# Attention without V: normalised probabilities on the input's rows, and one folded matrix per head

## The chip, the cores and the metric

One core of a Trainium2 chip runs the whole program. The metric is the device time of one execution in microseconds; smaller is better. Three runs of the kernel before took 1573.14 to 1573.82 us, 1573.54 in the median.

## The reference

The program is two layers on 8 sequences (batches) of 512 tokens of 128 features, in float32. Layer 0 is a Mamba block times the SiLU of a mixture of 24 experts. Layer 1, which the change touches, is causal attention times the SiLU of a mixture of 128 experts. Cut to the attention, per batch:

```python
xn = x / max(|x|, 1e-12) * sqrt(128) * gamma          # rows of 512 tokens
q, k, v = split(xn @ w_qkv.T)                         # 8 heads of 128
sim = (q * 128**-0.5) @ k.T                           # causal mask above the diagonal
attn = softmax(sim, axis=-1)
out = concat_heads(attn @ v) @ w_out.T                # 128 features again
```

As everything is linear in v, a head's share of `out` is attn @ xn @ (Wv.T Wo.T): the product of the two weight matrices can be made once per head.

## The kernel before

Layer 1 has two stages. `attention_input_stage` normalises the rows of x, scales them (`xa`, in a ring of four batches), transposes them (`xaT`, where gamma is multiplied in) and folds the weights on TensorE: M holds per head Wq.T Wk scaled by 128**-0.5, N holds per head Wv.T Wo.T. Both are 128 x 1024.

`attention_stage` then runs 64 heads (n = 8 b + h), in a loop on each engine that is written out by hand. An engine works strictly in the order of its own program; semaphores join the engines. For head n:

- TensorE `query(n)` makes M_h.T xaT in the bank `p_q` (two heads ahead); ScalarE `copy_query` takes it to `qT`.
- TensorE `score(n)` makes four tiles of rows against 128, 256, 384 or 512 keys, with the mask added by a bfloat16 product, in the order of `BANKS`: tile 3, then tiles 2 and 0, then tile 1.
- VectorE `maxima(n)` takes each tile's negated maximum; ScalarE `exps(n)` writes `pr` and the row sums (`sums`).
- TensorE `turn(n)` transposes the ten 128x128 blocks in three parts into two banks `p_t` (with `query(n + 2)` between the second and the third, which reuses the first part's bank); VectorE copies the parts to `pT`.
- TensorE `weigh(n)` makes the head's output in `p_o`: ten products of 128 columns, with blocks of pT as weights and V as the moving side. V is made by `value(k)` eight heads ahead, one 128x512 product per head through `p_q` (and `p_s` for the first eight, ahead of the first query), and copied by ScalarE (`copy_value`).
- VectorE `add_head(n)`, one head later, multiplies `p_o` by the reciprocal of the sums and adds it to `s_rows`. It counts `out_used`, for which the next `weigh` waits.

In float32 one product is two matmul instructions in the trace; a transpose is one.

Beside each loop runs the work of `Moe1` (`side_by_side`): at each `yield` of the main loop the engine takes one step of it. There are two yields per head. TensorE has them after `turn(n)` and after `score(n + 1)`, ScalarE after `exps(n)` with the copy behind it and after `copy_query(n + 2)`, and VectorE ahead of the copies to pT and ahead of `maxima(n + 1)`. So VectorE's order for head n is: maxima(n), side step, copies(n), add_head(n - 1), side step, maxima(n + 1). By step number the side work is: steps 0 to 15 `leaders` (the two best experts), 15 to 30 counting, 32 to 39 the one-hot tables, 40 the gates, 44 to 75 the expert products (TensorE, ScalarE), 84 to 107 `combine` on VectorE in two of three steps, 110 the SiLU of 4096 rows on ScalarE, and from 114 on, in every second step, one batch of the output: two 128x512 products on VectorE (`s_rows_added` is `out_used`), and its store. GpSimd makes masks and running counts beside steps 0 to 18 and issues the gathers later.

Of the kernel before, what the change touches and what calls it, by code (L numbers as in the profile page):

```python
# [24 lines left out]
P = 128  # L25
# [1652 lines left out]
NH = 8  # L1678
# [7 lines left out]

def attention_input_stage(nc, w, xn_dram, x_rows, xn_rows, xaT, M, N, loads):


    with ExitStack() as ctx:  # L1690
# [6 lines left out]
        xnT = s.sb("xnT", [P, 2, L])  # L1697
        xa = s.sb("xa", [P, 4, TB, D])
        qkv = s.sb("qkv", [P, 3 * NH, D])
# [47 lines left out]
        def _(dve):  # L1747
            link = Chain(dve, chain)
            v = nc.vector
            for g in range(B + 4):  # L1750
# [16 lines left out]
                if 2 <= g <= B + 1:  # L1767
                    b = g - 2
                    t = tiles(b)
                    dve.wait_ge(norm_ready, b + 1)  # L1770
                    link(v.tensor_scalar(l2[:, t], l2[:, t], 1e-12, float(D) ** -0.5, ALU.max, ALU.mult))
                    link(v.reciprocal(l2[:, t], l2[:, t]))
                    dve.wait_ge(normed, b + 1)
                    if b >= 4:
                        dve.wait_ge(a_turned, b - 3)
                    v.tensor_tensor(xa[:, b % 4, :, :], xn_rows[:, tiles(b), :], bcast(l2[:, tiles(b)], D),
                                    ALU.mult).then_inc(xa_ready, 1)
# [9 lines left out]
        def _(pe):  # L1787
# [8 lines left out]
            def turn_scaled(b):  # L1796
                pe.wait_ge(xa_ready, b + 1)
                if b >= 2:
                    pe.wait_ge(xaT_ready, b - 1)
                for j in range(TB):  # L1800
                    ins = nc.tensor.transpose(p_a[:, b % 2, j * P:(j + 1) * P], xa[:, b % 4, j, :], w["ident"])
                ins.then_inc(a_turned, 1)
# [34 lines left out]
        def _(act):  # L1837
            for g in range(B + 3):
# [33 lines left out]
def attention_stage(nc, w, xaT, M, N, s_rows, beside):  # L1872

# [4 lines left out]
    with ExitStack() as ctx:  # L1878
        s = Scope(nc, ctx, "at")
        qT = s.sb("qT", [P, 3, L])  # L1880
        V = s.sb("V", [P, 2, TB, NH * D])
        pr = s.sb("pr", [P, 2, 3, 512])
# [9 lines left out]
        q_copied = s.sem("q_copied")  # L1892
        v_product = s.sem("v_product")
        v_copied = s.sem("v_copied")
        scores = s.sem("scores")
        maxed = s.sem("maxed")
        exped = s.sem("exped")
        turned = s.sem("turned")
        pT_ready = s.sem("pT_ready")
# [8 lines left out]

        def value_bank(k):

            return p_s[:, k % 4, :] if k < NH and k % 4 < 3 else p_q[:, :]

        def tensor_steps(pe):
            def query(n):
                b, h = divmod(n, NH)
                pe.wait_ge(v_copied, min(NH * B, NH + max(n - 2, 0)))
                if n:
                    pe.wait_ge(q_copied, n)
                nc.tensor.matmul(p_q[:, :], M[:, h * D:(h + 1) * D], xaT[:, b, :], start=True,  # L1919
                                 stop=True).then_inc(q_product, 1)  # L1920

            def value(k):
                b, i = divmod(k, NH)
                t, half = divmod(i, 2)
                if k >= NH:
                    pe.wait_ge(v_copied, k)
                    pe.wait_ge(q_copied, min(NI, k - NH + 3))
                elif k >= 4:
                    pe.wait_ge(v_copied, k - 3)
                nc.tensor.matmul(value_bank(k), xaT[:, b, t * P:(t + 1) * P], N[:, half * 512:(half + 1) * 512],  # L1930
                                 start=True, stop=True).then_inc(v_product, 1)

# [33 lines left out]

            def weigh(n):
                b, h = divmod(n, NH)
                pe.wait_ge(v_copied, NH * (b + 1))
                if n:  # L1970
                    pe.wait_ge(out_used, n)
                pe.wait_ge(pT_ready, 3 * (n + 1))
                for i in range(TB):
                    for j in range(i + 1):
                        bank, c = PT_AT[j]
                        ins = nc.tensor.matmul(p_o[:, i, :], pT[:, n % 2, bank, c + (i - j) * P:c + (i - j + 1) * P],  # L1976
                                               V[:, b % 2, j, h * D:(h + 1) * D], start=(j == 0), stop=(j == i))
                ins.then_inc(out_ready, 1)

            for k in range(NH):  # L1980
                value(k)
            query(0)
            query(1)
            score(0)
            for n in range(NI):
                turn(n)
                yield
                if n + 1 < NI:
                    score(n + 1)
                yield  # L1990
                if n + NH < NI:
                    value(n + NH)
                weigh(n)

        def scalar_steps(act):
# [5 lines left out]

            def copy_value(k):
                b, i = divmod(k, NH)
                t, half = divmod(i, 2)
                act.wait_ge(v_product, k + 1)
                if b >= 2:
                    act.wait_ge(out_ready, NH * (b - 1))
                nc.scalar.activation(V[:, b % 2, t, half * 512:(half + 1) * 512], value_bank(k),
                                     ACT.Copy).then_inc(v_copied, 1)

            def exps(n):
                if n >= 2:
                    act.wait_ge(turned, 3 * (n - 1))
                if n >= 3:
                    act.wait_ge(out_used, n - 2)
                for k, tiles in enumerate(BANKS):
# [7 lines left out]

            for k in range(NH):
                copy_value(k)
            copy_query(0)
            copy_query(1)
            for n in range(NI):
                exps(n)  # L2030
                if n and n - 1 + NH < NI:
                    copy_value(n - 1 + NH)
                yield
                if n + 2 < NI:
                    copy_query(n + 2)
                yield

        def vector_steps(dve):
# [11 lines left out]

            def add_head(n):
                b, h = divmod(n, NH)
                link(v.reciprocal(sums[:, n % 3, :], sums[:, n % 3, :]))  # L2053
                dve.wait_ge(out_ready, n + 1)
                for i in range(TB):
                    o = s_rows[:, b * TB + i, :]
                    if h == 0:
                        ins = v.tensor_scalar(o, p_o[:, i, :], sums[:, n % 3, i:i + 1], None, ALU.mult)
                    else:
                        ins = v.scalar_tensor_tensor(out=o, in0=p_o[:, i, :], scalar=sums[:, n % 3, i:i + 1], in1=o,  # L2060
                                                     op0=ALU.mult, op1=ALU.add)
                ins.then_inc(out_used, 1)
# [39 lines left out]
class Moe1:  # L2102
# [262 lines left out]
    def vector(self, dve):  # L2365
# [111 lines left out]
        for b in range(B):  # L2477
            t = slice(b * TB, (b + 1) * TB)
            dve.wait_ge(self.g_ready, b // 2 + 1)
            dve.wait_ge(self.s_rows_added, NH * (b + 1))  # L2480
            link(v.tensor_tensor(self.o[:, t, :], self.o[:, t, :], self.s_rows[:, t, :], ALU.mult))
# [19 lines left out]
def program(nc, a, out):  # L2501

    with ExitStack() as top:
# [70 lines left out]
        with ExitStack() as l1:  # L2574
# [7 lines left out]
            w["qkv_dram"], w["wo_dram"] = a["qkv"], a["wo"]  # L2582
            A_ = Scope(nc, l1, "att")
            xaT = A_.sb("xaT", [P, B, L])
            M = A_.sb("M", [P, NH * D])
            N = A_.sb("N", [P, NH * D])
            attention_input_stage(nc, w, xn1_dram, rows, xn_rows, xaT, M, N, l1w)
            with ExitStack() as att:
                moe = Moe1(nc, att, w, r, xn_rows, xn1_dram, a["we"], y3_dram, s_rows, rows, out, outputs_stored)
                attention_stage(nc, w, xaT, M, N, s_rows, moe)  # L2590

# [75 lines left out]
```

## Time and profile before

| | us |
|---|---|
| median of three runs | 1573.54 |
| span of the profiled execution | 1568.1 |
| TensorE matmuls busy | 1331.6 (85%) |
| VectorE busy | 1253.2 (80%) |
| ScalarE busy | 848.2 (54%) |
| GpSimd busy | 650.5 (41%) |
| first instruction of the attention stage | 1027.07 |
| the 64 heads, from first transposes to the end | 1042.2 to 1568.1 |

The profiled execution gives no time of its own beside its span. In the attention stage TensorE is busy 522 of 541 us, at a granted clock of 0.99 to 1.00. A share that high over a stage says little about one head; the order of time within single heads says which engine the next one waits for.

### The profile page before, as it was taken

What the parts mean: (1) busy time and instruction counts of PE and PEld (TensorE: products, weight loads), DVE (VectorE), ACT (ScalarE), POOL (GpSimd) and SP (SyncE); (2) the same over time, 40 slices, a digit from 0 to 9 for tenths busy, and PEclk for the clock granted to TensorE, in tenths of its full rate; (3) what the DMA queues carried; (4) which work ended last, traced back from release to release, by engine and by line L of the source; (5) the groups of instructions that cost most, each with busy time, mean ns of one, the idle gap of its engine ahead of it and who ended that gap; (6) DMA issues with size and microseconds to landing.
All of it is one profiled execution on the core that took longest, in us unless ns stands there. A gap on an engine that the chain in (4) does not pass through costs nothing. (4 is left out here: it accounts for less than half of the span.)

```text
span 1568.1 us, 21870 instructions
## 1 busy us (share of the span) xinstructions
PE 1331.6 (85%) x7560; PEld 909.2 (58%) x7560; DVE 1253.2 (80%) x2263; ACT 848.2 (54%) x2090; POOL 650.5 (41%) x600
## 2 busy tenths in 40 slices
PE   7968788878987757899895696489999999999998
PEld 5534344443433336788784564356667677777776
DVE  6669989898889899999995857858988655567767
ACT  5367566565887765556551457553454444444452
POOL 0036554406798835545523755029600222146200
PEclk9979999888987958999997799699999999999999
DMA  6013455444343213545434210200010233112101
GB/s 215 0 29 106 128 142 143 122 117 135 106 135 121 94 59 105 144 128 139 130 95 154 56 35 2 98 15 1 1 39 17 55 84 102 40 33 47 22 15 41
DMA packets 75891, 127.31 MB, mean 81 GB/s; under 512 B 11758, under 2 KB 38606, under 8 KB 75174
## 3 DMA queue, kind: packets, MB, share of 16 engines
q1 hardware_dynamic: 56326, 75.04, 15.9%
q0 software_dynamic: 19456, 50.88, 12.2%
q8 instruction: 61, 1.00, 0.3%
q14 instruction: 48, 0.39, 0.1%
HBM read 85.51 MB, written 40.37 MB: 80 GB/s over the span
## 5 line engine op out<-in xcount | busy, mean ns | idle before, releaser
L643 DVE TENSOR_TENSOR_SCAN sc_st<-sc_dA,sc_st 128x1024 f32<-128x1024 f32 x128 | 293.2, 2331 | 0.0
L2070 DVE COPY at_pT<-at_p_t 128x512 f32<-128x512 f32 (+1 forms) x192 | 109.3, 599 | 132.4 <-PE at_p_t L1963 132.1
L2021 ACT ACTIVATE at_pr<-at_p_s,at_nmx 128x512 f32<-128x512 f32 (+3 forms) x256 | 131.3, 527 | 130.9 <-DVE at_nmx L2047 130.8
L1205 POOL DMA_INDIRECT g_state<-xn_scratch,moe_tab x96 | 116.1, 1209 | 183.6 <-POOLq L99 100.7
L613 DVE TENSOR_TENSOR sc_st<-sc_u,sc_p_b 128x1024 f32<-128x1024 f32 x128 | 154.9, 1210 | 45.2 <-PE sc_p_b L483 24.5
L422 ACT ACTIVATE sc_dA<-sc_dt,g_state 128x511 f32<-128x511 f32 x256 | 169.1, 710 | 16.2 <-DVE sc_st L643 12.7
L1942 PE MATMUL at_p_s<-att_xaT,at_qT 128*128 128x512 f32 (+3 forms) x512 | 172.0, 458 | 0.0
L1976 PEld LDWEIGHTS at_p_o<-at_V,at_pT 128*128 128x128 f32 x1280 | 152.4, 192 | 29.6 <-issue 28.8
L1236 POOL DMA_INDIRECT g_state<-r_scratch,moe_tab x96 | 114.2, 1189 | 113.8 <-PE e_bank L1335 79.7
L1976 PE MATMUL at_p_o<-at_V,at_pT 128*128 128x128 f32 x1280 | 153.7, 275 | 1.8 <-DVE g_state L2060 1.8
L621 DVE TENSOR_TENSOR sc_st<-sc_st,sc_p_c 128x1024 f32<-128x1024 f32 x128 | 155.1, 1212 | 0.0
L513 PEld LDWEIGHTS sc_p_y<-g_ident,sc_st 128*128 128x128 f32 x1024 | 133.2, 154 | 31.8 <-issue 21.1
L513 PE MATMUL sc_p_y<-g_ident,sc_st 128*128 128x128 f32 x1024 | 147.8, 292 | 3.3 <-DVE sc_st L621 3.3
L483 PE MATMUL sc_p_b<-sc_bc,mamba_sel 96*128 96x512 bf16 x128 | 55.3, 432 | 96.3 <-DVE sc_st L613 95.1
L2047 DVE TENSOR_REDUCE at_nmx<-at_p_s 128x1 f32<-128x512 f32 (+3 forms) x256 | 108.9, 481 | 20.1 <-PE at_p_s L1945 19.6
L1215 POOL DMA_INDIRECT g_state<-y_scratch,moe_back x64 | 87.2, 1363 | 84.6 <-DMA y_scratch<-g_state 52.2
L1287 PE MATMUL e_bank<-g_state 128*96 128x512 f32 x192 | 101.8, 632 | 8.6 <-ACT g_state L1349 8.6
L2238 POOL DMA_INDIRECT f_xg<-xn_scratch,l_tab x32 | 30.3, 946 | 184.6 <-DVE l_tab L2446 92.3
L1322 PE MATMUL e_bank<-g_state 128*96 128x128 f32 x768 | 102.2, 277 | 4.4 <-ACT g_state L1456 4.0
L1942 PEld LDWEIGHTS at_p_s<-att_xaT,at_qT 128*128 128x128 f32 x512 | 78.0, 191 | 41.0 <-issue 39.2
L1359 ACT ACTIVATE g_state<-e_bank 96x512 f32<-96x512 f32 x96 | 56.1, 589 | 82.7 <-PE e_bank L1287 82.3
L1963 PEld LDWEIGHTS at_p_t<-g_ident,at_pr 128*128 128x128 f32 x640 | 74.3, 141 | 45.7 <-DVE at_pT L2070 22.7
(296 smaller groups left out, 2739.6 us busy)
## 6 DMA issues: line engine op xcount, KB each, us to landing
y_scratch<-g_state SPq DMA_DIRECT2D x24, 768.0 KB, 5.3
g_state<-W SPq DMA_DIRECT2D x48, 256.0 KB, 5.3
r_scratch<-g_state SPq DMA_DIRECT2D x16, 512.0 KB, 2.6
y_scratch<-g_state SPq DMA_DIRECT2D x24, 192.0 KB, 3.1
xn_scratch<-g_state SPq DMA_DIRECT2D x16, 256.0 KB, 4.5
g_state<-x SPq DMA_DIRECT2D x4, 512.0 KB, 6.0
g_state<-xn_scratch SPq DMA_DIRECT2D x8, 256.0 KB, 6.0
g_state<-x SPq DMA_DIRECT2D x1, 2048.0 KB
```

The costliest lines, as they stand in the source:

```text
L422: ins = nc.scalar.activation(dA[:, m % 4, j, 1:L], dt[:, b % 2, h, 1:L], ACT.Exp, scale=negA[:, h, 2 * q + j:2 * q + j + 1])
L513: ins = nc.tensor.matmul(p_y[:, t, h * P:(h + 1) * P], st[:, (2 * i + h) % RS, j, t * P:(t + 1) * P], w["ident"], is_transpose=True, start ...
L613: nc.vector.tensor_tensor(st[:, m % RS:m % RS + 2, j, :], u[:, b % 2, :, :], p_b[:, :].unsqueeze(1).broadcast_to([P, HALF, L]), ALU.mult). ...
L621: nc.vector.tensor_tensor(st[:, m % RS, :, :], st[:, m % RS, :, :], p_c[:, :, :], ALU.mult).then_inc(hc_ready, 1)
L643: nc.vector.tensor_tensor_scan(st[:, m % RS, :, :].rearrange("p a b -> p (a b)"), dA[:, m % 4, :, :].rearrange("p a b -> p (a b)"), st[:, ...
L1205: nc.gpsimd.indirect_dma_start(out=self.xg[:, e % 4, h, :], out_offset=None, in_=self.xn_rows, in_offset=bass.IndirectOffsetOnAxis(ap=r.ta ...
L1236: nc.gpsimd.indirect_dma_start(out=self.rg[:, e % 3, h, :], out_offset=None, in_=self.r_rows, in_offset=bass.IndirectOffsetOnAxis(ap=r.tab ...
L1942: nc.tensor.matmul(p_s[:, bank, c:c + K], qT[:, n % 3, i * P:(i + 1) * P], xaT[:, b, 0:K], start=True, stop=False)
L1976: ins = nc.tensor.matmul(p_o[:, i, :], pT[:, n % 2, bank, c + (i - j) * P:c + (i - j + 1) * P], V[:, b % 2, j, h * D:(h + 1) * D], start=( ...
L2021: ins = nc.scalar.activation(pr[:, n % 2, bank, c:c + K], p_s[:, bank, c:c + K], ACT.Exp, bias=nmx[:, n % 2, i:i + 1], accum_out=sums[:, n ...
L2047: ins = v.tensor_reduce(nmx[:, n % 2, i:i + 1], p_s[:, bank, c:c + (i + 1) * P], AX_X, ALU.max, negate=True)
L2070: v.tensor_copy(pT[:, n % 2, part, 0:cols], p_t[:, PT_BANK[part], 0:cols]).then_inc(pT_ready, 1)
```

## The change

V goes. The probabilities are normalised before they are transposed: VectorE's `normalise(n)` waits for each part of the exps, takes the reciprocals of its sums one column at a time and multiplies the part's rows of `pr` in place; `turn(n)` waits for that (`scaled`). `weigh(n)` makes y.T = xa.T attn.T for all 512 rows in four products of 512, 384, 256 and 128 columns, with blocks of `xa` as weights and pT as the moving side, into `p_q`. ScalarE's `copy_weighed` takes it to `yT`, and `add_head(n - 1)` multiplies it with the head's N in four products of 128 columns, which sum over the eight heads of a batch in `p_o`. VectorE's `take_rows` copies a batch's sum once, one head after the batch's end. The rows `xa` of all batches stay in SBUF; gamma, which was in xaT and so in V, now scales N as well. `out_used` counts batches.

```diff
-                    v.tensor_tensor(xa[:, b % 4, :, :], xn_rows[:, tiles(b), :], bcast(l2[:, tiles(b)], D),
+                    v.tensor_tensor(xa[:, b, :, :], xn_rows[:, tiles(b), :], bcast(l2[:, tiles(b)], D),
...
-                                         scale=SCALE if n < 2 else 1.0).then_inc(fold_copied, 1)
+                                         scale=SCALE if n < 2 else w["gamma"]).then_inc(fold_copied, 1)
...
             def query(n):
                 b, h = divmod(n, NH)
-                pe.wait_ge(v_copied, min(NH * B, NH + max(n - 2, 0)))
-                if n:
+                if n >= 3:
+                    pe.wait_ge(y_copied, n - 2)
+                elif n:
                     pe.wait_ge(q_copied, n)
...
             def turn(n):
-                pe.wait_ge(exped, 3 * (n + 1))
+                pe.wait_ge(scaled, 3 * (n + 1))
...
             def weigh(n):
+                b = n // NH
+                pe.wait_ge(q_copied, min(n + 3, NI))
+                if n:
+                    pe.wait_ge(y_copied, n)
+                pe.wait_ge(pT_ready, 3 * (n + 1))
+                for j in range(TB):
+                    bank, c = PT_AT[j]
+                    ins = nc.tensor.matmul(p_q[:, j * P:L], xa[:, b, j, :], pT[:, n % 2, bank, c:c + (TB - j) * P],
+                                           start=(j == 0), stop=(j == TB - 1))
+                ins.then_inc(y_product, 1)
+
+            def add_head(n):
                 b, h = divmod(n, NH)
-                pe.wait_ge(v_copied, NH * (b + 1))
-                if n:
-                    pe.wait_ge(out_used, n)
-                pe.wait_ge(pT_ready, 3 * (n + 1))
+                pe.wait_ge(y_copied, n + 1)
+                if h == 0 and b:
+                    pe.wait_ge(out_used, b)
                 for i in range(TB):
-                    for j in range(i + 1):
-                        bank, c = PT_AT[j]
-                        ins = nc.tensor.matmul(p_o[:, i, :], pT[:, n % 2, bank, c + (i - j) * P:c + (i - j + 1) * P],
-                                               V[:, b % 2, j, h * D:(h + 1) * D], start=(j == 0), stop=(j == i))
+                    ins = nc.tensor.matmul(p_o[:, i, :], yT[:, n % 2, i * P:(i + 1) * P], N[:, h * D:(h + 1) * D],
+                                           start=(h == 0 and i == 0), stop=(h == NH - 1 and i == TB - 1))
                 ins.then_inc(out_ready, 1)
 
-            for k in range(NH):
-                value(k)
...
                 yield
-                if n + NH < NI:
-                    value(n + NH)
                 weigh(n)
+                if n:
+                    add_head(n - 1)
+            add_head(NI - 1)
...
+            def copy_weighed(n):
+                act.wait_ge(y_product, n + 1)
+                if n >= 2:
+                    act.wait_ge(out_ready, n - 1)
+                nc.scalar.activation(yT[:, n % 2, :], p_q[:, :], ACT.Copy).then_inc(y_copied, 1)
...
             for n in range(NI):
                 exps(n)
-                if n and n - 1 + NH < NI:
-                    copy_value(n - 1 + NH)
+                if n:
+                    copy_weighed(n - 1)
                 yield
...
+            def normalise(n):
+                for k, tiles in enumerate(BANKS):
+                    dve.wait_ge(exped, 3 * n + k + 1)
+                    for i in tiles:
+                        ins = v.reciprocal(sums[:, n % 3, i:i + 1], sums[:, n % 3, i:i + 1])
+                    link(ins)
+                    for i in tiles:
+                        bank, c = SIM_AT[i]
+                        row = pr[:, n % 2, bank, c:c + (i + 1) * P]
+                        ins = v.tensor_scalar(row, row, sums[:, n % 3, i:i + 1], None, ALU.mult)
+                    ins.then_inc(scaled, 1)
+
+            def take_rows(b):
+                dve.wait_ge(out_ready, NH * (b + 1))
+                v.tensor_copy(s_rows[:, b * TB:(b + 1) * TB, :], p_o[:, :, :]).then_inc(out_used, 1)
 
             maxima(0)
+            normalise(0)
             for n in range(NI):
                 yield
                 for part in range(3):
                     dve.wait_ge(turned, 3 * n + part + 1)
+                    if n >= 2:
+                        dve.wait_ge(y_product, n - 1)
                     cols = 512 if part < 2 else 256
                     v.tensor_copy(pT[:, n % 2, part, 0:cols], p_t[:, PT_BANK[part], 0:cols]).then_inc(pT_ready, 1)
-                if n > 1:
-                    dve.wait_ge(out_used, n - 1)
-                if n:
-                    add_head(n - 1)
+                if n > 1 and n % NH == 1:
+                    take_rows(n // NH - 1)
                 yield
                 if n + 1 < NI:
                     maxima(n + 1)
-            dve.wait_ge(out_used, NI - 1)
-            add_head(NI - 1)
+                    normalise(n + 1)
+            take_rows(B - 1)
```

## Rows read from the trace of the kernel before

**Rows 1.** The chain of waits in order of time: start us, us, what.

```profile
1027.07 2.81 PE at_p_s L1930 x6
...
1034.87 1.14 PE at_p_q L1919 x2
...
1066.32 1.09 PE at_p_t L1963 x8
...
1074.69 1.09 PE at_p_t L1963 x8
...
1541.43 2.29 PE at_p_o L1976 x20
1548.22 2.29 PE at_p_o L1976 x20
```

**Rows 2.** A timeline of TensorE, head 41: start us, us, engine, line, operation.

```profile
1390.95 1.04 PE L1963 MATMUL at_p_t<-g_ident,at_pr 128*128 128x128 f32 x8
...
1392.90 1.03 PE L1942 MATMUL at_p_s<-att_xaT,at_qT 128*128 128x512 f32 x2
...
1395.45 1.08 PE L1930 MATMUL at_p_q<-att_N,att_xaT 128*128 128x512 f32 x2
1396.36 2.40 PE L1976 MATMUL at_p_o<-at_V,at_pT 128*128 128x128 f32 x20
1398.59 1.04 PE L1963 MATMUL at_p_t<-g_ident,at_pr 128*128 128x128 f32 x8
```

**Rows 3.** The same head on VectorE (first row) and ScalarE, same columns.

```profile
1394.68 1.68 DVE L2047 TENSOR_REDUCE at_nmx<-at_p_s 128x1 f32<-128x512 f32 x4
...
1395.48 0.69 ACT L2021 ACTIVATE at_pr<-at_p_s,at_nmx 128x512 f32<-128x512 f32 x1 [2.00 <-DVE at_nmx L2047]
...
1396.96 0.21 ACT L2021 ACTIVATION_READ_ACCUMULATOR at_pr<-at_p_s,at_nmx 128x1 f32 x1
...
1397.41 0.21 ACT L2021 ACTIVATION_READ_ACCUMULATOR at_pr<-at_p_s,at_nmx 128x1 f32 x1
```

**Rows 4.** A head with experts beside it, all engines in order of time.

```profile
1308.07 1.04 PE L1963 MATMUL at_p_t<-g_ident,at_pr 128*128 128x128 f32 x8
...
1310.69 1.12 PE L1942 MATMUL at_p_s<-att_xaT,at_qT 128*128 128x512 f32 x2
...
1311.91 0.69 DVE L2047 TENSOR_REDUCE at_nmx<-at_p_s 128x1 f32<-128x512 f32 x1
...
1313.00 1.09 DVE L2047 TENSOR_REDUCE at_nmx<-at_p_s 128x1 f32<-128x384 f32 x3 [0.40 <-PE at_p_s L1945]
...
1313.76 0.38 ACT L2346 ACTIVATE f_xgT<-f_bank 128x256 f32<-128x256 f32 x1 [2.06 <-PE f_bank L2308]
...
1314.04 0.68 ACT L2021 ACTIVATE at_pr<-at_p_s,at_nmx 128x512 f32<-128x512 f32 x1
...
1316.65 1.04 PE L1963 MATMUL at_p_t<-g_ident,at_pr 128*128 128x128 f32 x8
```

**Rows 5.** Groups by form (busy us, mean ns), and two lines by source (min/median/max).

```profile
L2070 DVE COPY at_pT<-at_p_t 128x512 f32<-128x512 f32 x128 | 82.4, 686 | 119.7 <-PE at_p_t L1963 119.7
...
L2070 DVE COPY at_pT<-at_p_t 128x256 f32<-128x256 f32 x64 | 27.2, 424 | 12.6 <-PE at_p_t L1963 12.4 <-issue 0.2
...
L2053 DVE RECIPROCAL at_sums<-at_sums 128x4 f32<-128x4 f32 x64 | 10.7, 168 | 0.0
...
L2058 DVE TENSOR_SCALAR g_state<-at_p_o,at_sums 128x128 f32<-128x128 f32 x32 | 9.0, 344 | 0.3
...
L2452 DVE TENSOR_SCALAR g_state<-f_m,l_wk x32: 272/279/398, 1396.3 to 1484.4; 128x128 f32<-128x128 f32 x32
...
L2379 DVE CAST f_idx<-f_ix x8: 171/436/453, 1045.9 to 1104.8; 128x8 f32<-128x8 uint32 x8
```

**Rows 6.** A timeline of head 3, the side step and the maxima on VectorE.

```profile
1070.11 0.48 DVE L2372 MAX8 f_mx<-g_state 128x8 f32<-128x128 f32 x2
...
1071.70 1.67 DVE L2047 TENSOR_REDUCE at_nmx<-at_p_s 128x1 f32<-128x512 f32 x4
```

More of the change, by code:

```diff
@@ L1684, with attention_input_stage @@
 PT_BANK = (0, 1, 0)
-def attention_input_stage(nc, w, xn_dram, x_rows, xn_rows, xaT, M, N, loads):
+def attention_input_stage(nc, w, xn_dram, x_rows, xn_rows, xa, xaT, M, N, loads):
     with ExitStack() as ctx:
@@ L1697, in attention_input_stage @@
         xnT = s.sb("xnT", [P, 2, L])
-        xa = s.sb("xa", [P, 4, TB, D])
         qkv = s.sb("qkv", [P, 3 * NH, D])
@@ L1800, in turn_scaled @@
                 for j in range(TB):
-                    ins = nc.tensor.transpose(p_a[:, b % 2, j * P:(j + 1) * P], xa[:, b % 4, j, :], w["ident"])
+                    ins = nc.tensor.transpose(p_a[:, b % 2, j * P:(j + 1) * P], xa[:, b, j, :], w["ident"])
                 ins.then_inc(a_turned, 1)
@@ L1868, in _, with attention_stage @@
                     nc.scalar.activation(dst, p_w[:, n % 2, :], ACT.Copy,
-                                         scale=SCALE if n < 2 else 1.0).then_inc(fold_copied, 1)
-def attention_stage(nc, w, xaT, M, N, s_rows, beside):
+                                         scale=SCALE if n < 2 else w["gamma"]).then_inc(fold_copied, 1)
+def attention_stage(nc, w, xa, xaT, M, N, s_rows, beside):
     NI = B * NH
@@ L1880, in attention_stage @@
         qT = s.sb("qT", [P, 3, L])
-        V = s.sb("V", [P, 2, TB, NH * D])
+        yT = s.sb("yT", [P, 2, L])
         pr = s.sb("pr", [P, 2, 3, 512])
@@ L1892, in attention_stage @@
         q_copied = s.sem("q_copied")
-        v_product = s.sem("v_product")
-        v_copied = s.sem("v_copied")
+        y_product = s.sem("y_product")
+        y_copied = s.sem("y_copied")
         scores = s.sem("scores")
@@ L1897, in attention_stage @@
         exped = s.sem("exped")
+        scaled = s.sem("scaled")
         turned = s.sem("turned")
@@ L1903, in attention_stage @@
         block = ctx.enter_context(nc.Block())
-        def value_bank(k):
-            return p_s[:, k % 4, :] if k < NH and k % 4 < 3 else p_q[:, :]
         def tensor_steps(pe):
@@ L1920, in query @@
                                  stop=True).then_inc(q_product, 1)
[L1922 to L1931, printed above, removed]
             def score(n):
@@ L2014, in exps @@
                 if n >= 3:
-                    act.wait_ge(out_used, n - 2)
+                    act.wait_ge(scaled, 3 * (n - 2))
                 for k, tiles in enumerate(BANKS):
@@ L2023, in exps @@
                     ins.then_inc(exped, 1)
-            for k in range(NH):
-                copy_value(k)
             copy_query(0)
@@ L2036, in scalar_steps @@
                 yield
+            copy_weighed(NI - 1)
         def vector_steps(dve):
@@ L2049, in maxima @@
                     ins.then_inc(maxed, 1)
[L2051 to L2062, printed above, removed]
+            def normalise(n):
[12 more added lines that the diff above has]
+                v.tensor_copy(s_rows[:, b * TB:(b + 1) * TB, :], p_o[:, :, :]).then_inc(out_used, 1)
             maxima(0)
+            normalise(0)
             for n in range(NI):
@@ L2479, in vector @@
             dve.wait_ge(self.g_ready, b // 2 + 1)
-            dve.wait_ge(self.s_rows_added, NH * (b + 1))
+            dve.wait_ge(self.s_rows_added, b + 1)
             link(v.tensor_tensor(self.o[:, t, :], self.o[:, t, :], self.s_rows[:, t, :], ALU.mult))
@@ L2583, in program @@
             A_ = Scope(nc, l1, "att")
+            xa = A_.sb("xa", [P, B, TB, D])
             xaT = A_.sb("xaT", [P, B, L])
@@ L2586, in program @@
             N = A_.sb("N", [P, NH * D])
-            attention_input_stage(nc, w, xn1_dram, rows, xn_rows, xaT, M, N, l1w)
+            attention_input_stage(nc, w, xn1_dram, rows, xn_rows, xa, xaT, M, N, l1w)
             with ExitStack() as att:
                 moe = Moe1(nc, att, w, r, xn_rows, xn1_dram, a["we"], y3_dram, s_rows, rows, out, outputs_stored)
-                attention_stage(nc, w, xaT, M, N, s_rows, moe)
+                attention_stage(nc, w, xa, xaT, M, N, s_rows, moe)
 def laid_out(i):
```

10 lines of the change are left out of this document (removed).

## The prediction

> **What bounds the kernel now.** I read the chain of waits first: the attention stage starts with the value products at 1027.07 and lasts to the end, 541 us of 1568.1. Its chain shows a step that repeats for each of the 64 heads, so I cut it into heads by TensorE's first transposes (time T, `turn`) and by its first score product (time S). Then I read three heads in order of time. The heads from 37 to 54 have nothing beside them on TensorE, and one of them takes 7.64 us, from 1390.95 to 1398.59 [rows 2]: TensorE's work in it joins without a gap, the value product takes 0.91 of it (1395.45 to 1396.36) and `weigh` 2.23. Beside it ScalarE's exps run from 1395.48 to 1397.62 [rows 3], so the next transposes could have started 0.97 us earlier. That 0.97 is the only room for new work between exp and transpose. In the 15 heads that carry Moe1's experts a head takes 8.58 us (1308.07 to 1316.65) [rows 4]: ScalarE must first copy Moe1's turned rows at 1313.76, so its exps start at 1314.04, 3.35 after S, not 2.58, and end at about 1316.2: room 0.47. In heads 0 to 6 the side work is VectorE's `leaders`, and the chain goes through VectorE and ScalarE: 8.37 us (1066.32 to 1074.69) [rows 1]. In heads 56 to 62 there are no values left: 6.79 us (1541.43 to 1548.22) [rows 1].
>
> **TensorE's share of the change.** Columns decide. `weigh` keeps 1280 float32 columns (ten of 128 become 512+384+256+128), and `add_head`, four of 128, adds the 512 that the value product had. The 20 passes of `weigh` are 111 ns apart (2.23/20) [rows 2]. In the wide form there are 8 passes, and the 0.02 to 0.1 us that the small ones lose goes: I take 2.16 for `weigh` and 0.89 for `add_head` (8 passes at 111). 3.14 becomes 3.05, a gain of 0.09 per head, between 0 and 0.2. TensorE's own head is then 7.56. The loads of weights, 20 to 16 per head, already lie beside matmuls. The Trainium skill ("TensorE: Matmul & The Clock Gate", what each phase is for) says that time is purely the moving columns and that weight loads are pulled ahead; rows 2 agree, 1280 columns in 2.23, and by that rule fewer and wider products win next to nothing.
>
> But values were computed only until head 55 and eight of them ahead of the first query, while `add_head` runs in all 64 heads. Start: the first query goes from 1034.87 to 1027.07, -7.8 [rows 1]; the first head's scaling gives back 1.0 (below): **-6.8**. End: heads 56 to 62 carried no value product and now carry `add_head`.
>
> **The new wait.** `turn` waited for exp; now it waits for `scaled`, VectorE's reciprocals and four multiplications in place. What they cost: a reciprocal of four columns is 0.168, and one of one column can't be much less; with the wait behind it 0.20, two in a row 0.28 [rows 5]. A multiplication of 128 columns from SBUF to SBUF takes 0.279 (median), from PSUM 0.344 [rows 5]: the difference is 0.064. Copies from PSUM take 0.424 for 256 columns and 0.686 for 512 [rows 5], 1.02 ns per column, 0.131 for 128; so the one from SBUF is as much shorter as it would be at half that time per column. I take 0.51 ns: 0.28 for 128, 0.35 for 256, 0.41 for 384, 0.48 for 512, each overlapping the next by 0.08. The other bound is the PSUM rate: 0.34, 0.42 and 0.56 for 128, 256 and 384 columns. The Trainium skill ("VectorE: DVE Perf Modes", the perf-mode tier table) gives a tensor_scalar of float32 in SBUF twice the rate of one from PSUM at best; the difference of 0.064 agrees, and the sum by it is the sum I make.
> With X the start of the exps, the 128-column exp ends (its accumulator read, 1396.96+0.21) at X+1.69 [rows 3]. From there: semaphore 0.05, two reciprocals 0.28, 384 columns 0.34, 128 columns 0.28, last reciprocal 0.20 less 0.08 of overlap, 256 columns 0.35, semaphore 0.07: T' = X+3.2. The last exp ended at X+2.14, so 1.0 us is added behind the exps (floor 0.6: only the last reciprocal and multiplication; at the PSUM rate: 1.35).
>
> **Heads with experts.** T to S 2.62 (1308.07 to 1310.69), and 0.06 more as TensorE now starts from idle; S to X 3.35; X to T' 3.2 [rows 4]. Together 9.2, against 8.58, while TensorE's sum falls to 8.49. 15 heads by 0.65: **+9.8** (floor 0.6 in place of 1.0: +3.8).
>
> **Bare heads (21, 37 to 54).** VectorE's four accumulations leave the stretch before the maxima, which therefore start when scores land: S+1.22 and S+2.31 (1311.91, 1313.00 against 1310.69) [rows 4], not S+1.78 (1394.68) [rows 3]. X = S+2.02, but the second exp waits for its maximum until S+3.05, ends with the 128 at S+4.06, and T' = S+5.57; with T to S 1.95 that makes 7.52, just below TensorE's 7.56. The new wait is covered here, by 0.04 us. 19 heads by -0.1: **-1.9**. If the cover is gone, each 0.1 of longer scaling costs 2 us over these heads.
>
> **VectorE's side work moves onto the path.** A side step used to run between the maxima and the copies to pT, with VectorE idle behind it; now it sits behind `normalise`, that is, at T, when TensorE's transposes are about to be copied. The bank of the first transposes is needed again by the last two, so TensorE waits for the copy: S = T + max(1.95, B+0.84) with B the side work: it starts at T-0.13 (semaphore and overlap), the copy takes 0.69 and a semaphore 0.06, the last two transposes 0.22.
> - Heads 56 to 62: the output's two 128x512 products, B about 1.33 (two passes of 0.686 [rows 5], less one overlap). S = T+2.17, and behind it TensorE has 5.6: 7.78, against 6.79. With head 56 bare (7.56): **+6.7**.
> - Heads 0 to 6: from T to the maxima was 5.38 (1071.70 - 1066.32), 1.24 of it the reciprocal and accumulations that go, and the `leaders` of 1.59 that stay (1070.11 to 1071.70) [rows 6]. The copies lose 0.02. So T+4.16, 0.8 to the exps, 3.2 to the transposes: 8.16, against 8.37. But GpSimd is busy here. A cast in SBUF takes 0.171 at least and 0.436 in the median [rows 5], so up to 0.27 for each of the two or three multiplications behind the last exps: 0.55 more. 7 heads by +0.33: **+2.3** (-1.5 to +4.5).
> - Heads 7 to 9 (side steps of two kinds at once; two passes of 512 columns and one of 1024, 2.6 us by 1.02 ns per column, ahead of the copies): 1.8 by the same sum, an estimate, and 1.6 for GpSimd: **+3.4**. Heads 10 to 19 are TensorE's with counting beside, the copy costs 0.2 of stall less 0.09: **+1.0**. Head 20 (the gates, seven small operations of some 0.2 to 0.35 each, estimated at 1.95): **+0.7**.
>
> **ScalarE and the rest.** `copy_weighed` is the size of the copy it replaces and ends by T, before the query at T+0.87 needs p_q. The table changes around head 55's SiLU put its exps on the path: the full **+1.0**. Tail: `weigh` starts earlier, but its copy, `add_head` and a 128x512 copy follow in series: **+0.4**. In the input stage gamma moves to a copy that has a scale anyway, and a wait goes: nothing. `out_used` now counts batches, with no reader near.
>
> **Sum.** -6.8+2.3+3.4+1.0+0.7+9.8-1.9+1.0+6.7+0.4 = +16.6 us on the span: 1584.7. The median of the runs (1573.5) is 5.4 above the profiled span, which is the only time that the profile gives of its execution: **1590.1 us**.
>
> **Rivals.**
> - *All hidden (faster).* The scaling keeps up with the exps, so that less than 0.4 us is left behind them, under the 0.47 of the expert heads. Then every head is TensorE's: -7.8, 64 by -0.09, +5.3 for `add_head` in the last seven, and about -2 where VectorE led: 1563. For it: VectorE is idle while ScalarE works, 3 us per head. Against: the last reciprocal and multiplication can't start before the last exp. 7 in 100.
> - *Small remainder.* The floor of 0.6, no trouble with GpSimd: 26 heads by -0.4 and -4: 1576 to 1580. 13 in 100.
> - *The PSUM rate.* 1.35 in place of 1.0; the bare heads' cover goes too: 26 by 0.35 and 30 by 0.3: 1608. Against it the 0.279. 8 in 100.
> - *GpSimd's port.* Every multiplication waits for a whole GpSimd instruction, 0.4 to 0.6 us in heads 0 to 9, and 2.8 where one of those is that long: +8, 1598. The cast row speaks for it, but eight columns in one place are all there is. 12 in 100. The Trainium skill ("SBUF — State Buffer", two separate sides) says that a two-port VectorE operation and a GpSimd one exclude each other for a whole instruction; the cast agrees in direction, and no row shows it for a multiplication.
> - *Doesn't do what it says.* The wide products could run slower per column than I take; then `weigh` stays at 2.23 and all bare heads cost what they did: +2, 1592, inside the forecast.
>
> The forecast itself has 60 in 100, with 1583 to 1597 as its own range; 80 in 100 need 1577 to 1603. A run can tell 0.2% (3.1 us) from no change: faster 0.08, same 0.05, slower 0.87.
>
> **What would show it.** Right: expert heads at 9.1 to 9.3 with TensorE idle before the transposes, released by VectorE's multiplication; bare heads at 7.5 to 7.6 without that idle time; the last heads at 7.8; the first query at 1027. Wrong: multiplications of 384 columns at 0.6, the idle time released by ScalarE, or GpSimd's or the tail's waits above 1 us.

## The result, and the profile after

The changed kernel takes 1582.59 us in the median of 20 runs against 1572.64 for the kernel before, run beside it; the ratio is 1.0056 with a 95% interval of 1.0029 to 1.0083, so 4.6 to 13.1 us more. The profiled span is 1580.5 us, 12.4 more than before.

The spans need one word of care. Profiles differ in the stages ahead of attention by up to 16 us although the code there is the same (the attention stage begins at 1016.4 in the profile of e2 below and at 1032.0 in that of e5), while the interval from one head to the next repeats within 0.04 us. So I compare the heads' intervals, from first transposes to first transposes, and use whole times only with their intervals. Of the 12.4 us, 1.3 lie ahead of the attention stage, where nothing of weight changed.

The chain of waits of the changed kernel, in order of time, shows the start and two heads with experts, in the columns of [rows 1]:

```profile
1028.35 1.11 PE at_p_q L1914 x2
...
1236.86 1.09 PE at_p_t L1947 x8
...
1246.10 1.09 PE at_p_t L1947 x8
```

The stage now begins with the query; its first transposes come 8.18 us later, where the kernel before took 15.15. They wait for VectorE's multiplication too, as the timeline shows:

```profile
1036.53 1.09 PE L1947 MATMUL at_p_t<-g_ident,at_pr 128*128 128x128 f32 x8 [2.72 <-DVE at_pr L2048]
```

A head with experts takes 9.23 to 9.24 us, against 8.58 [rows 4].

What ends it is seen in one such head, all engines, columns as in [rows 4]:

```profile
1310.68 1.09 PE L1947 MATMUL at_p_t<-g_ident,at_pr 128*128 128x128 f32 x8 [0.46 <-DVE at_pr L2048]
...
1313.36 1.13 PE L1926 MATMUL at_p_s<-att_xaT,at_qT 128*128 128x512 f32 x2
...
1316.44 0.38 ACT L2338 ACTIVATE f_xgT<-f_bank 128x256 f32<-128x256 f32 x1 [2.07 <-PE f_bank L2300]
...
1316.72 0.68 ACT L2010 ACTIVATE at_pr<-at_p_s,at_nmx 128x512 f32<-128x512 f32 x1
...
1318.70 0.70 DVE L2048 TENSOR_SCALAR at_pr<-at_pr,at_sums 128x384 f32<-128x384 f32 x2
...
1319.51 0.35 DVE L2048 TENSOR_SCALAR at_pr<-at_pr,at_sums 128x256 f32<-128x256 f32 x1
1319.91 0.77 PE L1947 MATMUL at_p_t<-g_ident,at_pr 128*128 128x128 f32 x5 [0.46 <-DVE at_pr L2048]
```

TensorE idles 0.46 us ahead of the transposes of such a head and is released by VectorE's multiplication. From the start of the exps (1316.72) to the transposes (1319.91) it is 3.19 us; from the first score product (S) to the exps 3.36; from the first transposes (T) to S 2.68.

The same kernel in bare head 41, which answers to [rows 2, 3]:

```profile
1397.14 1.04 PE L1947 MATMUL at_p_t<-g_ident,at_pr 128*128 128x128 f32 x8
...
1401.64 2.38 PE L1959 MATMUL at_p_q<-at_pT,att_xa 128*128 128x512 f32 x8
...
1403.85 1.06 PE L1969 MATMUL at_p_o<-att_N,at_yT 128*128 128x128 f32 x8
...
1404.12 0.35 DVE L2048 TENSOR_SCALAR at_pr<-at_pr,at_sums 128x256 f32<-128x256 f32 x1
...
1404.74 0.49 PE L1947 MATMUL at_p_t<-g_ident,at_pr 128*128 128x128 f32 x3
```

Here no engine holds TensorE up. The four wide products take 2.21 us (1401.64 to 1403.85), the ten small ones took 2.23 (1396.36 to 1398.59) [rows 2]: next to nothing is won by the width. The last multiplication ends at 1404.47, 0.27 ahead of the transposes.

All 64 heads in one table; each interval runs from one head's first transposes to the next head's, and the intervals of a group are added up, us. Heads 38 to 54 have no experts; beside some of them VectorE combines the experts' rows:

| part | before | after | difference | forecast |
|---|---|---|---|---|
| stage's start to first transposes | 15.15 | 8.18 | -7.0 | -6.8 |
| heads 0 to 6 | 57.65 | 56.48 | -1.2 | +2.3 |
| heads 7 to 9 | 28.18 | 32.74 | +4.6 | +3.4 |
| heads 10 to 19 | 86.68 | 85.49 | -1.2 | +1.0 |
| head 20 | 7.65 | 8.09 | +0.4 | +0.7 |
| heads 22 to 37 (experts) | 137.98 | 147.39 | +9.4 | +9.8 |
| heads 21, 38 to 54 (bare, combine) | 140.19 | 138.58 | -1.6 | -1.9 |
| head 55 (SiLU) | 8.72 | 10.02 | +1.3 | +1.0 |
| heads 56 to 62 | 47.57 | 53.51 | +5.9 | +6.7 |
| last head to the end | 11.30 | 11.69 | +0.4 | +0.4 |
| attention stage | 541.07 | 552.17 | +11.1 | +16.6 |

### The profile page after: what moved, and what is told of

The parts are those of the page before. It is cut to its first block and busy times, and to the rows that moved or that the text cites. A ratio compares the mean times of both kernels' runs of the same rounds, so it can differ in the third digit from the quotient of the medians.

```text
span 1580.5 us, 21312 instructions
## 1 busy us (share of the span) xinstructions
PE 1332.9 (84%) x7176; PEld 886.6 (56%) x7176; DVE 1306.0 (83%) x2463; ACT 855.1 (54%) x2090; POOL 656.5 (42%) x600
## 5 line engine op out<-in xcount | busy, mean ns | idle before, releaser
L1959 PE MATMUL at_p_q<-at_pT,att_xa 128*128 128x512 f32 (+3 forms) x512 | 150.9, 438 | 1.6 <-ACT at_qT L1992 1.0
L1959 PEld LDWEIGHTS at_p_q<-at_pT,att_xa 128*128 128x128 f32 x512 | 92.9, 190 | 58.3 <-issue 31.4
L1947 PE MATMUL at_p_t<-g_ident,at_pr 128*128 128x128 f32 x640 | 93.9, 278 | 22.2 <-DVE at_pr L2048 17.6
L2048 DVE TENSOR_SCALAR at_pr<-at_pr,at_sums 128x512 f32<-128x512 f32 (+3 forms) x256 | 99.9, 411 | 6.8
```

The lines of the kernel that those rows point to most:

```text
L1947: ins = nc.tensor.transpose(p_t[:, bank, c + (i - j) * P:c + (i - j + 1) * P], pr[:, n % 2, sbank, sc + j * P:sc + (j + 1) * P], w["ident"])
L1959: ins = nc.tensor.matmul(p_q[:, j * P:L], xa[:, b, j, :], pT[:, n % 2, bank, c:c + (TB - j) * P], start=(j == 0), stop=(j == TB - 1))
L2048: ins = v.tensor_scalar(row, row, sums[:, n % 3, i:i + 1], None, ALU.mult)
```

## The experiments

**Without the scaling (e1).** What would the new data flow cost without its new wait and VectorE's time for it? The kernel leaves the scaling out, and the probabilities stay unnormalised. ScalarE's wait before it writes `pr` again moves to the product that has read it.

```diff
-                pe.wait_ge(scaled, 3 * (n + 1))
+                pe.wait_ge(exped, 3 * (n + 1))
...
-                    act.wait_ge(scaled, 3 * (n - 2))
+                    act.wait_ge(y_product, n - 2)
...
-            normalise(0)
...
                     maxima(n + 1)
-                    normalise(n + 1)
```

> The changed kernel without its normalisation: the reciprocals and multiplications are left out and the transposes wait for the exps; the output is that of unnormalised probabilities. Theory (the loss is the new wait behind the exps, and VectorE's time for it): the heads with experts go from 9.23 to TensorE's own 8.55 us, heads 7 to 9 lose some 6 us together, heads 0 to 6 fall to about 7.6 to 7.8, head 55 to about 9.0; bare heads stay at 7.61 and heads 57 to 62 at 7.64. In all some 19 us less than the changed kernel, 6 to 8 us less than the kernel before (ratio about 0.995). Rival (the loss is in the wide products and the head's own product on TensorE, or in copy_weighed): the heads with experts stay above 9, the ratio stays near 1.006.

Measured: ratio 0.991 (0.9863 to 0.9957), 7 to 22 us less than before. Heads with experts 8.55 us, heads 7 to 9 together 26.6 (32.7 in the changed kernel), 0 to 6 52.5 (56.5), 55 9.1, and the bare heads stay at 7.61. From the first transposes of head 0 to those of head 63 it is 507.1 us; the changed kernel has 532.3 and the kernel before 514.6. The scaling costs 25 us there, more than the 19 expected (heads 0 to 6, 10 to 19 and 42 to 54 give back 7 us together, of which I had counted 3), and everything else together is a gain. The rival, that the products cost the time, falls. The run takes the wait and VectorE's work away together; e3 and e5 tell the two apart.

**The turned rows later (e3, e4).** In heads with experts ScalarE copies the experts' turned rows ahead of the exps. The edit puts that copy into the next side step, in the changed kernel (e3) and in the kernel before (e4):

```diff
-        copy_turned(0)
         for q in range(self.NP):
+            copy_turned(q)
             act.wait_ge(self.product, q + 1)
...
             yield
-            if q + 1 < self.NP:
-                copy_turned(q + 1)
             yield
```

> The changed kernel, with ScalarE's copy of the experts' turned rows moved from ahead of the exps to the next side step, behind them. Theory (in heads with experts the exps start late because of this copy, and the scaling behind them then has no cover): 9.23 falls to TensorE's 8.55 us in 15 heads, 10 us in all, and the ratio to before to about 1.000. Rival (the scaling itself is longer than its cover wherever the exps start): the heads stay above 8.9.

> The kernel before with the same move. Theory: there the late exps were covered (0.47 us of room), so its heads with experts stay at 8.58 and the ratio is 1.000. Rival (the move takes work off the path of both kernels): 8.3 or less, ratio 0.997.

Measured: e3 1.0022 (0.9989 to 1.0055), its heads with experts 8.55 us where they had 9.23, and 522.1 us from head 0 to head 63, 10.2 less than the changed kernel. e4 1.0015 (0.9984 to 1.0046), its heads 8.59, as before. A head of e3, same columns:

```profile
1318.70 0.69 ACT L2010 ACTIVATE at_pr<-at_p_s,at_nmx 128x512 f32<-128x512 f32 x1 [1.02 <-DVE at_nmx L2035]
...
1321.81 0.35 DVE L2048 TENSOR_SCALAR at_pr<-at_pr,at_sums 128x256 f32<-128x256 f32 x1
...
1322.40 0.38 ACT L2338 ACTIVATE f_xgT<-f_bank 128x256 f32<-128x256 f32 x1
...
1322.60 0.82 PE L1947 MATMUL at_p_t<-g_ident,at_pr 128*128 128x128 f32 x6
```

The exps wait for the maxima again and start 2.02 us after S (1316.68), not 3.36; the multiplication ends 0.44 us ahead of the transposes, and the copy runs at 1322.40, where nobody needs ScalarE. The same scaling costs 0.68 us per head or nothing, depending on when the exps start. In the kernel before the late exps cost nothing, so moving them gains nothing.

**A second multiplication of the last 256 columns (e5).**

```diff
+                    if k == 2:
+                        link(ins)
+                        ins = v.tensor_scalar(row, row, 1.0, None, ALU.mult)
                     ins.then_inc(scaled, 1)
```

> The changed kernel with a second multiplication, by one, of the last 256 columns (0.35 us and a wait). Theory (in heads with experts nothing covers the scaling; in bare heads TensorE covers it with 0.25 us to spare): heads with experts 9.23 to about 9.6, bare heads 7.61 to about 7.75, heads 57 to 62 7.64 to about 7.75, heads 0 to 6 up by 0.35. Rival (the scaling is hidden in both, and the experts' heads are long for another reason): no head changes.

Measured: heads with experts 9.55 (+0.32), bare heads 7.78 (+0.17) except head 38 with 7.85 and head 39 with 8.13, heads 57 to 62 7.97 (+0.33); head 0 to head 63 17 us more. The direction is as expected, but the cover is thinner: 0.15 us in bare heads, not 0.25, and none in the last heads, where VectorE's side step follows the scaling and the copies follow the side step. A multiplication that ends 0.27 us ahead of the transposes does not leave 0.27 us of room: in the bare heads of e5 0.06 us lie between the last multiplication and the transposes, and the first copy starts 0.69 us after T, where the changed kernel has 0.64. These 0.11 and the cover of 0.15 make up the 0.27 to 0.01 us.

**Tile by tile (e6).** Each of the four row tiles is scaled when its own exp ends.

```diff
-                    ins.then_inc(exped, 1)
+                        ins.then_inc(exped, 1)
...
-                    dve.wait_ge(exped, 3 * n + k + 1)
                     for i in tiles:
-                        ins = v.reciprocal(sums[:, n % 3, i:i + 1], sums[:, n % 3, i:i + 1])
-                    link(ins)
-                    for i in tiles:
+                        dve.wait_ge(exped, 4 * n + (3, 2, 0, 1).index(i) + 1)
+                        link(v.reciprocal(sums[:, n % 3, i:i + 1], sums[:, n % 3, i:i + 1]))
```

> The changed kernel, with each row tile scaled when its own exp ends, not when its part of the exps does. Theory (the scaling's remainder behind the last exp is made of the work that waits for the second part): the interval from the start of the exps to the transposes falls by about 0.2 us, the heads with experts from 9.23 to about 9.0, bare heads stay at 7.61. Rival (only the last multiplication counts): 9.2.

Measured: heads with experts 8.96 us (9.23), heads 42 to 48 7.61 to 7.62 (up to 7.82 in the changed kernel), bare heads 7.61. The rival falls: 0.27 us of the remainder were work that waited for the second part of the exps.

**Shorter GpSimd operations (e2).** The long interval in the changed kernel is the 13.39 us from head 8's transposes to head 9's. VectorE in it, and GpSimd below:

```profile
1109.50 1.67 DVE L2035 TENSOR_REDUCE at_nmx<-at_p_s 128x1 f32<-128x512 f32 x4
...
1111.31 0.94 DVE L2048 TENSOR_SCALAR at_pr<-at_pr,at_sums 128x512 f32<-128x512 f32 x1
...
1112.41 1.39 DVE L2048 TENSOR_SCALAR at_pr<-at_pr,at_sums 128x384 f32<-128x384 f32 x2
...
1113.86 1.89 DVE L2048 TENSOR_SCALAR at_pr<-at_pr,at_sums 128x256 f32<-128x256 f32 x1
...
1110.85 2.87 POOL L2219 TENSOR_SCALAR f_R<-f_mh,g_pcol 128x1024 bf16<-128x1024 bf16 x1
1113.69 1.91 POOL L2220 TENSOR_TENSOR f_R<-f_mh,g_iota 128x1024 bf16<-128x1024 bf16 x1
```

The three rows take 0.49, 0.62 to 0.70 and 0.35 in most other heads. e2 cuts both GpSimd operations into eight pieces, the one-input one like this and the two-input one likewise:

```diff
-            nc.gpsimd.tensor_scalar(self.R[k][:, :, 0, :], self.mh[k][:, :, :], w["pcol"], None, ALU.mult)
+            for t in range(0, NT, 4):
+                nc.gpsimd.tensor_scalar(self.R[k][:, t:t + 4, 0, :], self.mh[k][:, t:t + 4, :], w["pcol"], None,
+                                        ALU.mult)
...
```

> The changed kernel, with GpSimd's four long operations for the tables (128x1024, 2.9 and 1.9 us each) cut into eight pieces each. Theory (VectorE's two-port multiplications wait for a whole GpSimd operation): the multiplications of head 9, which took up to 1.89 us, fall to at most 0.8, and the interval from head 8 to head 9, 13.39 us, to 10.5 to 11. Rival (the interval is long because of VectorE's own side work in that head): it stays above 12.5.

Measured: 11.10 us, the multiplications 0.61, 0.73 and 0.35. The next head lost 0.26, so 2.0 us are gained in all. The rival is right about the rest: with its side work the interval stays long at 11.1, and heads 7 to 9 together stay 2.5 us longer than in the kernel before (30.70 to 28.18).

**More GpSimd work of either kind (e9b, e10b), and the same beside the kernel before (e11b).** In the rows above the multiplications of 512 and 384 columns end inside the one-input operation, while the last one ends after the two-input operation. e9b makes the one-input operation six times in place of once; e10b, and e11b in the kernel before, repeat the two-input one as shown (harmlessly, each makes the same values again):

```diff
+            for _ in range(8):
+                link(nc.gpsimd.tensor_tensor(self.R[k][:, :, 1, :], self.mh[k][:, :, :],
+                                             bcast(iota[:, 0:NT], self.HI), ALU.mult))
```

> The changed kernel, with GpSimd's one-input 128x1024 multiplication (2.87 us) made six times in place of once, twice, so that it runs some 34 us beside heads 9 to 13. In the changed kernel VectorE's 512-column multiplication took 0.94 beside such an operation, not 0.49, and did not wait for its end. Theory A (one-input GpSimd operations slow VectorE's two-port ones to the one-port time, no more): the multiplications there take 0.6 to 1.0 us, the heads 10 to 13 go from 8.8 to 9.2 to 9.8. Theory B (each waits for a whole GpSimd operation): up to 2.9 us for one, heads above 12.

> The changed kernel, with GpSimd's two-input 128x1024 multiplication (1.91 us) made nine times in place of once, twice: some 31 us more beside heads 9 to 13. In the changed kernel the multiplication of 1.89 us began 0.17 after such an operation and ended 0.15 after it. Theory B (a VectorE multiplication waits for a whole two-input operation): single multiplications of 1 to 2.2 us, heads 10 to 13 at 11 to 14 us. Theory A (it is only slowed): at most 1.0 us for one, heads at 9.2 to 9.8.

> The same GpSimd operations in the kernel before, where VectorE's per-head work reads PSUM or is a reduction. Theory (only VectorE operations that use two ports or two inputs in SBUF meet GpSimd): heads 10 to 13 stay at 8.45 to 8.89 us. Rival (GpSimd's traffic slows all of VectorE): they rise by 0.5 us or more.

Measured, intervals that begin with heads 8 to 12: changed kernel 13.40, 9.95, 8.78, 8.79, 8.84; e9b 12.70, 10.35, 10.02, 9.58, 9.21; e10b 13.38, 14.86, 14.71, 10.29, 8.84. e11b is the kernel before to 0.02 us. VectorE and GpSimd in e9b, then in e10b:

```profile
1112.99 1.02 DVE L2048 TENSOR_SCALAR at_pr<-at_pr,at_sums 128x384 f32<-128x384 f32 x2
...
1114.11 0.35 DVE L2048 TENSOR_SCALAR at_pr<-at_pr,at_sums 128x256 f32<-128x256 f32 x1
...
1120.73 0.92 DVE L2048 TENSOR_SCALAR at_pr<-at_pr,at_sums 128x512 f32<-128x512 f32 x1
...
1123.27 1.21 DVE L2048 TENSOR_SCALAR at_pr<-at_pr,at_sums 128x256 f32<-128x256 f32 x1
...
1112.43 2.92 POOL L2220 TENSOR_SCALAR f_R<-f_mh,g_pcol 128x1024 bf16<-128x1024 bf16 x1
...
1123.22 2.84 POOL L2220 TENSOR_SCALAR f_R<-f_mh,g_pcol 128x1024 bf16<-128x1024 bf16 x1
```

```profile
1126.75 3.59 DVE L2048 TENSOR_SCALAR at_pr<-at_pr,at_sums 128x384 f32<-128x384 f32 x2
...
1130.44 1.95 DVE L2048 TENSOR_SCALAR at_pr<-at_pr,at_sums 128x256 f32<-128x256 f32 x1
...
1115.48 16.76 POOL L2221 TENSOR_TENSOR f_R<-f_mh,g_iota 128x1024 bf16<-128x1024 bf16 x8
1132.32 1.91 POOL L2223 TENSOR_TENSOR f_R<-f_mh,g_iota 128x1024 bf16<-128x1024 bf16 x1
```

Beside two-input operations theory B holds: a multiplication waits for whole ones. 1130.44 + 1.95 = 1132.39 lies 0.15 after the end of the eighth (1115.48 + 16.76), and all multiplications beside them end 0.08 to 0.28 after the end of one, the later the more columns they have (128: 0.09, 256: 0.15, 384: 0.22, 512: 0.28).

Beside one-input operations neither theory holds. None waits for a whole operation of 2.84 to 2.92 us (B), but they are not slowed to a rate either (A): 256 columns take 1.21 us at 1123.27 and their usual 0.35 at 1114.11. What decides is when they begin. Those that began in the first 0.6 us of a GpSimd operation ended 1.25 (256 columns) to 1.40 us (512 columns) after its start; less the 0.15 to 0.28 us that the same widths need after the end of a two-input operation, they were let in 1.10 to 1.16 us after its start, an estimate from these rows. Those that began 1.3 to 1.7 us after its start took their usual time. And the four in e9b that began 1.8 us after it or later ended 0.07 to 0.28 us after its end; the 128 columns inside the row at 1121.82 (1.05 us in place of 0.28) are one of them. So the 0.9 to 1.3 us are waits for a part of the operation. VectorE's copies and accumulations from PSUM and its maxima in e11b meet the same GpSimd work as in e10b and lose nothing: of the 81 VectorE operations in heads 9 to 13 none differs by more than 0.01 us from the kernel before.

**Value products to the end (e8).** The kernel before, with a product that nobody reads in its last eight heads.

```diff
+                else:
+                    pe.wait_ge(q_copied, min(NI, n + 3))
+                    nc.tensor.matmul(p_q[:, :], xaT[:, B - 1, 0:P], N[:, 0:512], start=True, stop=True)
```

> The kernel before, with a value product that nobody reads in the last eight heads too, where it had none. Theory (the last heads of the changed kernel are longer only because TensorE has the head's own product in them): these heads go from 6.8 to about 7.65 us, six to seven us in all. Rival (it is VectorE's side step ahead of the copies, or copy_weighed): they stay below 7.2.

Measured: 7.70 us in head 56 and 7.65 in heads 57 to 61, 5.7 us in all. The changed kernel has 7.66 and 7.64, so the product on TensorE alone accounts for 5.7 of its 5.9 us, and the rivals fall. Together with e5: in these heads TensorE and VectorE's chain of scaling, side step and copies are equally long within 0.03 us.

**All three together (e7).** The later copy (e3), the short GpSimd operations (e2) and the scaling tile by tile (e6).

> The changed kernel with the short GpSimd operations, the later copy of the turned rows, and the scaling tile by tile. Theory: experts' heads 8.55 (-10 us), head 8 near 10.6 (-3), the VectorE-led heads 0 to 9 by 0.2 less (-2): some 15 us under the changed kernel, 2 to 4 us under the kernel before, ratio 0.998. Rival (the three are not separate costs): a gain of 10 us or less, ratio above 1.000.

Measured: ratio 0.9967 (0.9934 to 1.0000), 1566.05 us in the median of 12. From head 0 to head 63 516.3 us: 16.0 less than the changed kernel, 1.7 more than before, and the start is 7 us shorter. Heads with experts 8.55, head 8 10.8. The attention stage takes 535.9 us, against 541.1 before and 552.2 in the changed kernel. The interval lies wholly below that of the changed kernel (1.0029 to 1.0083); against the kernel before the gain is 0 to 10 us, at the edge of what can be told from none.

## Why the prediction was right, and where its sizes were off

The direction, the main term and the engines named for it came out as written. The number was 7.5 us high: 1582.59 lies just below the forecast's own range of 1583 to 1597 and inside the wider one of 1577 to 1603. Of the 7.5 us, 4.2 are the span (1584.7 for 1580.5). The other 3.3 are the step from span to time: I added 5.4, the median of three runs less one profiled span, but the profiled execution of the changed kernel took 1582.71 us at its span of 1580.5, a step of 2.2, and in every run here it is between 1.7 and 3.1. The rest of the 5.4 must be that the profiled execution of the kernel before was shorter than the median one; its own time is not known.

- *The new wait.* Forecast: exps to transposes 3.2 us, heads with experts 9.2. Measured 3.19 and 9.23, with TensorE idle and released by the multiplication. The rate of 0.51 ns per column holds: the 256-column multiplication takes 0.35 as worked out. The floor of 0.6 and the PSUM rate are out. e1 and e3 show both halves of the argument, that the scaling is the cost, and that in heads with experts it costs only because the exps are late.
- *TensorE's share.* I gave the wide products 2.16 us; they take 2.21. So a bare head is 7.61, not 7.56, and the gain per head 0.04, not 0.09. The cover of the new wait there is 0.15 us (e5), where the sum gave 0.04. The first of the eight passes follows the bfloat16 mask and starts 0.06 after it (1401.58 to 1401.64), as score products do; I had left that out.
- *Start, tail, head 55, last heads.* Within 0.3 us each, but for the last heads: +5.9 for +6.7. I let VectorE's side step begin at T-0.13 and stall the copies. In fact the scaling ends 0.27 ahead of TensorE there, so the side step starts earlier and the stall is 0.04 (7.64 against 7.61). e5 shows that nothing more was left: 0.33 us more of scaling are 0.33 us more per head.
- *Heads 10 to 19* (+1.0, measured -1.2) fail in two steps. In heads 10 to 14 (+0.2) it is the same one: I took T as the end of the scaling also where TensorE sets T. In heads 11 to 14 the scaling ends up to 0.73 us ahead of T, and the stall of 0.2 is not there: they take 8.79 to 8.84 us, as they do without the scaling (e1). Only head 10 pays, 8.78 for 8.41 in e1. In heads 15 to 19 (-1.4) I had called TensorE the bound of the kernel before, and it wasn't. Its chain ran through the accumulations that the change takes away:

```profile
1200.71 0.86 DVE g_state L2060 x3
1201.56 1.21 DVE f_A L2401 x2
...
1202.82 0.41 PE f_bank L2295 x8
```

  That is one of them, in order of time: TensorE's side product waited for VectorE's `f_A`, and that for the accumulations. Heads 16 to 19 took 8.49 to 8.55; without them 8.18 are left (e1), 8.18 to 8.30 with the scaling.
- *GpSimd's port.* This term was mis-sized, and at the wrong place. I spread 0.55 us over each of heads 0 to 9. In heads 0 to 6 the 384 and 128 columns together take 0.68 to 1.05, 0.80 in the mean, where they take 0.62 alone, so about 0.2 per head; no run shows that this is GpSimd's doing. As the seven heads came to -1.2 with it, the rest of their sum, -1.5, would have had to be some -2.5 (an estimate: -1.2 less seven times 0.18), and why is open. In the interval before head 9 the term alone is 2.3 (e2), because there, and only there, a VectorE multiplication meets long GpSimd operations. Its last multiplication took 1.89 in place of 0.35: a wait above 1 us, which I had set down as a sign of being wrong, did appear in this one head. With short GpSimd operations 2.5 us are left in heads 7 to 9 (e2), where I had 1.8 for the side work. From one cast of eight columns I could not tell that the kind of GpSimd operation matters.

The sum of the stage was +16.6 and is +11.1; 3.5 of the 5.5 us are heads 0 to 6, 2.2 heads 10 to 19. The 12.4 us of the span lie inside the interval of the ratio, the forecast 16.6 above it.

Of the rivals, *all hidden* needed less than 0.4 us behind the exps; it is 1.04 (1318.87 to 1319.91). e3 hides the scaling in the heads with experts too, but by earlier exps and not by a shorter remainder. The Trainium skill's rule on wide products ("TensorE: Matmul & The Clock Gate", what each phase is for), that the moving columns set the time, agrees: 1280 columns take 2.21 us in 8 passes and 2.23 in 20. Its rule on the port ("SBUF — State Buffer", two separate sides), that the loser waits for a whole instruction, holds for two-input GpSimd operations (1.95 us for one of 0.35) and not for one-input ones, where a multiplication of 0.35 ended after 1.21 us, 1.26 after the start of an operation of 2.84 us. The measurement decides here.

## What to carry to other kernels

When the number of moving columns stays, fusing small products into wide ones gave TensorE almost nothing here (0.02 of 2.23 us); count what the new order of operations puts between two engines instead. A wait that moves onto a path is paid only where the engine that sets the pace has no other work: look for the head, or stage, with the smallest room, and ask what delays it there, since removing that (a copy that could run elsewhere) can be cheaper than making the new work faster. And follow where each engine's side work comes to lie after a reordering; the end of the new step is not the start of the next engine's.

## What the runs showed of the hardware

- VectorE's in-place multiplications in SBUF and GpSimd (whose own times are rougher in the profile): beside a two-input GpSimd operation (128x1024, 1.91 us) they wait for its end, 1.89 to 1.95 us for 256 columns in place of 0.35. Beside a one-input one (128x1024, 2.87 us) they are let in about 1.1 us after its start, run at their usual speed when begun 1.3 to 1.7 us after it, and wait for its end when begun later than 1.8: 0.92 us for 512 columns in place of 0.49, 1.21 for 256. A two-input VectorE operation waits as well: in e6 a 128x1024 comparison took 2.81 us in place of 1.23, GpSimd's two-input one ending at 1117.05:

```profile
1115.32 2.81 DVE L2391 TENSOR_TENSOR f_mh<-g_iota,f_hi_e 128x1024 bf16<-128x1024 f32 x1
...
1115.14 1.91 POOL L2218 TENSOR_TENSOR f_R<-f_mh,g_iota 128x1024 bf16<-128x1024 bf16 x1
```

- A small shift in time decides who meets whom: e6 left the GpSimd operations as they were, and the long interval moved from 13.39 us before head 9 to 11.49 there and 13.18 before head 10.
- The earlier stages of the same code differ by up to 16 us between profiled executions. In the four profiles whose attention stage begins at 1015.9 to 1017.4 (e2, e4, e8, e9b) the granted clock of TensorE from 300 to 500 us is 0.91 to 0.92 in the mean, in the nine others (1027.1 to 1032.0) 0.88. Which is cause and which effect is open; no run was made for it.
